# Cross attention in a six-layer kernel: V mixed for twelve chunks at a time, K stacked in pieces of 512 keys

## The reference

```python
Q = _proj(layernorm(x), Wq, bq)          # 256 x 16 x 32
K = _proj(ctx, Wk, bk); V = _proj(ctx, Wv, bv)   # 25088 x 16 x 32
scores = jnp.einsum('bihd,bjhd->bijh', Q, K) * SCALE
attn = jax.nn.softmax(scores, axis=1)    # over the 256 queries, for each key and head
x = jnp.einsum('bijh,bjhd->bihd', attn, V).reshape(B, S, D_MODEL)
return x @ Wo + bo
```

## Time and profile before

| | |
|---|---|
| median of 3 runs | 2509.08 us (2507.33 to 2509.38) |
| profiled execution | 2507.43 us |
| its span | 2505.7 us |
| granted TensorE clock, mean | 0.999 |
| PE busy | 2474.8 us, 99% |
| DVE, ACT, POOL busy | 77%, 73%, 48% |
| 16 DMA engines, SP's queue | 65.0% |

### The profile page before, as it was taken

How to read it: one execution, slowest core, us unless ns; L and a number is a source line. 1 busy time by engine, 2 the same in 40 slices (tenths; PEclk the granted TensorE clock), 3 DMA queues, 4 the chain that set the end, 5 groups by cost and what they waited for, 6 DMA issues and landing times.

```text
span 2505.7 us, 53166 instructions
## 1 busy us (share of the span) xinstructions
PE 2474.8 (99%) x18114; PEld 1993.9 (80%) x18114; DVE 1940.5 (77%) x3672; ACT 1827.4 (73%) x6877; POOL 1204.4 (48%) x1973
## 2 busy tenths in 40 slices
PE   8999999999999999999999999999999999999998
PEld 6876999877777777777777777777777777588897
DVE  8886866587778788877878777778788887669855
ACT  2214444288888888888888888888888888649743
POOL 5533111265555656555555565565556554430022
PEclk9999999999999999999999999999999999999999
DMA  9995545567676666766766776676676666348751
GB/s 391 386 373 212 196 185 190 130 175 171 167 171 165 165 164 163 176 162 164 174 161 166 170 169 167 163 169 166 163 178 163 163 156 136 152 162 333 289 200 44
DMA packets 138033, 472.98 MB, mean 189 GB/s; under 512 B 32664, under 2 KB 32792, under 8 KB 126368
## 3 DMA queue, kind: packets, MB, share of 16 engines
q1 hardware_dynamic: 130512, 456.20, 65.0%
q10 hardware_dynamic: 7248, 13.37, 1.4%
HBM read 244.53 MB, written 17.30 MB: 104 GB/s over the span
## 4 chain that ended last, share of the span: by engine, by line
PE 95%; DVE 2%; ACT 1%; DMA 1%; issue 0%; POOL 0%; SPq 0%; DVEq 0%
PE PB L816 21%; PE PB L846 15%; PE PB L834 14%; PE PB L857 14%; PE PB L776 6%; PE PB L622 6%; PE PB L956 4%; PE PB L971 3%; PE PB L789 3%; PE PB L1032 2%; PE PB L1058 2%; ACT EE L1264 1%; PE PB L665 1%; DMA AR<-in_ctx 1%; PE PB L722 1%; PE PB L672 1%
## 5 line engine op out<-in xcount | busy, mean ns | idle before, releaser
L1264 ACT ACTIVATE EE<-PB,small 128x256 f32<-128x256 f32 x3136 | 1435.8, 498 | 205.0 <-DVE small L1711 196.9
L1711 DVE TENSOR_REDUCE small<-PB 128x2 f32<-128x512 f32 x1568 | 1028.4, 683 | 314.5 <-PE PB L846 310.8
L1264 ACT ACTIVATION_READ_ACCUMULATOR EE<-PB,small 128x1 f32 x3136 | 721.3, 230 | 0.0
L846 PEld LDWEIGHTS PB<-QS,STK 128*128 128x128 f32 x3136 | 557.7, 188 | 175.0 <-issue 44.4
L816 PE MATMUL PB<-CTX,WKV 128*128 128x512 f32 x2352 | 680.8, 394 | 0.0
L2116 POOL TENSOR_TENSOR VS<-V,small 128x128 f32<-128x128 f32 x784 | 331.3, 423 | 676.1 <-DVE small L1717 676.1
L846 PE MATMUL PB<-QS,STK 128*128 128x256 f32 x3136 | 617.1, 285 | 3.2 <-ACT EE L1264 3.0
L834 PE MATMUL PB<-WKV,CTX 128*128 128x512 f32 x1584 | 469.2, 393 | 0.0
L816 PEld LDWEIGHTS PB<-CTX,WKV 128*128 128x128 f32 x2352 | 385.0, 189 | 29.7
L857 PE MATMUL PB<-EE,VS 128*32 128x256 f32 x6272 | 367.4, 381 | 1.0 <-POOL VS L2116 1.0
L857 PEld LDWEIGHTS PB<-EE,VS 128*32 128x32 f32 x6272 | 189.5, 110 | 131.3 <-POOL VS L2116 2.8
(11 more groups left out here) (287 smaller groups left out, 2385.3 us busy)
## 6 DMA issues: line engine op xcount, KB each, us to landing
STK<-KHL SPq DMA_DIRECT2D x1568, 128.0 KB, 2.4
RW<-in_l1f SPq DMA_DIRECT2D x64, 1024.0 KB, 5.7
AR<-in_ctx SPq DMA_DIRECT2D x49, 1024.0 KB, 8.2
RAW<-in_ctx SPq DMA_DIRECT2D x98, 512.0 KB, 3.8
WF<-in_l0f SPq DMA_DIRECT2D x17, 2304.0 KB, 9.0
V<-v_scr SPq DMA_DIRECT2D x64, 256.0 KB, 3.0
v_scr<-RAW ACTq DMA_DIRECT2D x49, 256.0 KB, 7.4
RW<-in_l1a SPq DMA_DIRECT2D x1, 4096.0 KB, 13.5
```

The lines of the kernel that those rows point to most:

```text
L846: m = e.matmul(bank(2 * (k % 2) + half, 256 * (s % 2), 256), STK[:, g % 2, s, c % 2, j:j + 128], QS[:, s, c, :], start=True, stop=True)
L1264: m = e.activation(EE[:, b, s, :], bank(2 * (k % 2) + half, 256 * (s % 2), 256), ACT.Exp, bias=nm[:, b, s:s + 1], accum_out=su[:, b, s:s + 1])
L1711: e.tensor_reduce(nm[:, k % RING, 2 * half:2 * half + 2], bank(2 * (k % 2) + half).rearrange("p (s i) -> p s i", s=2), axis=AX.X, op=ALU.m ...
```

## The change

Three things are changed together.

1. MIX goes from 6 to 12 and RING from 8 to 14. There is a batch of mixes after every twelfth chunk, and one more, of what is left, at the last chunk before TAIL.
2. K is no longer stacked in pairs: KHL, STK and KR hold one unit where they held two (KHL and STK still two in turn, KR one). `stack_k` runs for each unit, at k % 4 == 3, with 16 DMAs of half the size. Units are projected two ahead instead of four, and the context is loaded and split one group of 256 keys later. `k_raw` waits for the low part of the unit just before it.
3. OT and WO have no place of their own any more: OT lies in a slot of EE, WO in four slots of V, and W_o's load waits for V's last reader there. The last 16 chunks run in the plain order (`LAST_ORDER` goes), and the late V projections in `LATE_V` are moved some chunks forward.

```diff
-MIX = 6
-RING = 8
+MIX = 12
+RING = 14
...
-HEADS_DONE = [LAST + LAST_ORDER.index((3, c1 - 1)) + 1 for c0, c1 in HEADS_OUT]
+HEADS_DONE = [LAST + 4 * c1 for c0, c1 in HEADS_OUT]
+BATCH_ENDS = [k for k in range(TAIL) if k % MIX == MIX - 1 or k == TAIL - 1]
...
-    if k < LAST:
-        return 4 * (k // 16) + k % 4, k % 16 // 4
-    j, c = LAST_ORDER[k - LAST]
-    return NT - 4 + j, c
+    return 4 * (k // 16) + k % 4, k % 16 // 4
...
-    u = (k + AHEAD) // 4 + 4
+    u = (k + AHEAD) // 4 + 2
...
-        KHL = sb("KHL", [P, 2, 2, 2, CW], F32R, life)
-        STK = sb("STK", [P, 2, 4, 2, CW], F32R, life)
+        KHL = sb("KHL", [P, 2, 2, CW], F32R, life)
+        STK = sb("STK", [P, 2, 4, CW], F32R, life)
...
-        KR = sb("KR", [P, 2, CW], over=life)
+        KR = sb("KR", [P, CW], over=life)
...
+        OT, WO = EE[:, (NCH - 14) % RING], V[:, 4:8, :]
...
-            def stack_k(g):
-                if g >= 2:
-                    w.wait_ge("s_mm", 16 * (g - 2) + 16)
+            def stack_k(u):
+                if u >= 2:
+                    w.wait_ge("s_mm", 8 * (u - 2) + 8)
                 for part in range(2):
-                    w.wait_ge(*k_done(g, part))
+                    w.wait_ge(*k_done(u, part))
                     for s in range(4):
                         for q in (part, part + 2):
                             e.dma_start(
-                                STK[32 * q:32 * q + 32, g % 2, s, :, :].bitcast(F32),
-                                KHL[32 * s:32 * s + 32, g % 2, part, :, :].bitcast(F32)).then_inc(S[f"d_s{g % 2}"], 16)
+                                STK[32 * q:32 * q + 32, u % 2, s, :].bitcast(F32),
+                                KHL[32 * s:32 * s + 32, u % 2, part, :].bitcast(F32)).then_inc(S[f"d_s{u % 2}"], 16)
...
-                if k % 8 == 7 and g + 2 < NG:
-                    stack_k(g + 2)
-                if k % 8 == 5 and g + 7 < NG:
-                    load_ctx(g + 7)
+                if k % 4 == 3 and k // 4 + 2 < 2 * NG:
+                    stack_k(k // 4 + 2)
+                if k % 8 == 5 and g + 6 < NG:
+                    load_ctx(g + 6)
...
-            w.wait_ge("d_s1", 256 * NPAIR)
+            w.wait_ge("vs", NCH - 16)
...
-                first, last = k % MIX == 0, k % MIX == MIX - 1
+                first, last = k == 0 or k - 1 in BATCH_ENDS, k in BATCH_ENDS
...
-                if k % MIX == MIX - 1:
-                    for n in range(max(k - MIX - 1, 0), k - 1):
+                if last:
+                    for n in range(mixed, k - 1):
                         mix(n)
+                    mixed = k - 1
...
-                if (k + AHEAD) % 8 in (2, 3, 4, 5) and (k + AHEAD) // 8 + 4 < NG:
-                    split_lo((k + AHEAD) // 8 + 4, ((2, 3, 4, 5).index((k + AHEAD) % 8),))
+                if (k + AHEAD) % 8 in (2, 3, 4, 5) and (k + AHEAD) // 8 + 3 < NG:
+                    split_lo((k + AHEAD) // 8 + 3, ((2, 3, 4, 5).index((k + AHEAD) % 8),))
```

More of the change, by code:

```diff
@@ L388, in build, with k_done @@
         qf = EE[:, 3].rearrange("p c i -> p (c i)")
-        nm, su, rc = (small[:, o:o + 4 * RING].rearrange("p (b s) -> p b s", b=RING) for o in (0, 32, 64))
-        KBANK = (6, 7, 6, 3)
+        nm, su, rc = (small[:, o:o + 4 * RING].rearrange("p (b s) -> p b s", b=RING) for o in (0, 64, 128))
+        KBANK = (6, 7)
         VBANK = {1: 7, 2: 6}
-        def k_done(g, part):
-            return (("k_hi", "k_lo")[part], 2 * g + 2) if g < 2 else (("kr_hi", "kr_lo")[part], (1, 2)[part] * (2 * (g - 2) + 2))
+        def k_done(u, part):
+            return (("k_hi", "k_lo")[part], u + 1) if u < 2 else (("kr_hi", "kr_lo")[part], (1, 2)[part] * (u - 1))
         WS1 = (WSA, WSB)
@@ L840, in scores @@
                 t, c = chunk(k)
-                g, j = 2 * (t // 4) + c // 2, 128 * (t % 4)
-                w.wait_ge(f"d_s{g % 2}", 256 * (g // 2 + 1))
+                u, j = 4 * (t // 4) + c, 128 * (t % 4)
+                w.wait_ge(f"d_s{u % 2}", 256 * (u // 2 + 1))
                 if k >= 2:
@@ L845, in scores @@
                 for s in (2 * half, 2 * half + 1):
-                    m = e.matmul(bank(2 * (k % 2) + half, 256 * (s % 2), 256), STK[:, g % 2, s, c % 2, j:j + 128],
+                    m = e.matmul(bank(2 * (k % 2) + half, 256 * (s % 2), 256), STK[:, u % 2, s, j:j + 128],
                                  QS[:, s, c, :], start=True, stop=True)
@@ L884, in project @@
                 if u and steps:
-                    if steps[0] == 0 and u > 4:
-                        w.wait_ge("kr_out", u - 4)
+                    if steps[0] == 0 and u > 2:
+                        w.wait_ge("kr_out", u - 2)
                     project_k(u, steps=steps)
@@ L1254, in k_hi @@
                 w.wait_ge("kp_mm", u + 1)
-                e.activation(KHL[:, u // 2, 0, u % 2, :], bank(KBANK[u]), ACT.Identity,
+                e.activation(KHL[:, u, 0, :], bank(KBANK[u]), ACT.Identity,
                              bias=BC[:, C_L1XK + u:C_L1XK + u + 1]).then_inc(S["k_hi"], 1)
@@ L1270, in scalar_program @@
             move_xt(3)
-            for u in range(2, 4):
-                k_hi(u)
-                w.wait_ge("q_split", 1)
-                stack_q(e, 3, ((0, 1), (2, 3))[u - 2])
+            w.wait_ge("q_split", 1)
+            stack_q(e, 3, range(4))
             for k in range(NCH):
@@ L1690, in k_lo @@
                 e.scalar_tensor_tensor(
-                    out=KHL[:, u // 2, 1, u % 2, :], in0=bank(KBANK[u]), scalar=BC[:, C_L1XK + u:C_L1XK + u + 1],
-                    in1=KHL[:, u // 2, 0, u % 2, :].bitcast(F32), op0=ALU.add, op1=ALU.subtract).then_inc(S["k_lo"], 1)
+                    out=KHL[:, u, 1, :], in0=bank(KBANK[u]), scalar=BC[:, C_L1XK + u:C_L1XK + u + 1],
+                    in1=KHL[:, u, 0, :].bitcast(F32), op0=ALU.add, op1=ALU.subtract).then_inc(S["k_lo"], 1)
             def k_raw(u):
-                n, ch = u - 4, u % 4
+                n, ch = u - 2, u % 4
                 w.wait_ge("kp_mm", u + 1)
-                if n >= 2:
-                    w.wait_ge("kr_lo", 2 * (n - 1))
-                e.tensor_scalar(KR[:, n % 2, :], bank(4), BC[:, C_L1XK + ch:C_L1XK + ch + 1], None,
+                if n >= 1:
+                    w.wait_ge("kr_lo", 2 * n)
+                e.tensor_scalar(KR[:, :], bank(4), BC[:, C_L1XK + ch:C_L1XK + ch + 1], None,
                                 ALU.add).then_inc(S["kr_out"], 1)
@@ L1746, in vector_program @@
             e.tensor_tensor(hl[1], qf, hl[0].bitcast(F32), ALU.subtract).then_inc(S["q_split"], 1)
-            for u in range(2, 4):
-                k_lo(u)
-            split_hi(3)
             for n in range(3):
                 v_out(n)
-            split_hi(4, (0,))
+            split_hi(3, (0,))
             for k in range(NCH):
@@ L1766, in vector_program @@
                     e.tensor_tensor(X[:, k - 8, :], X[:, k - 8, :], BI[:, BSLOT[R_XO], :], ALU.add).then_inc(S["x_xbias"], 1)
-                if (k + AHEAD) % 8 in (0, 4) and (k + AHEAD) // 8 + 4 < NG:
-                    split_hi((k + AHEAD) // 8 + 4, ((0, 4).index((k + AHEAD) % 8),))
+                if (k + AHEAD) % 8 in (0, 4) and (k + AHEAD) // 8 + 3 < NG:
+                    split_hi((k + AHEAD) // 8 + 3, ((0, 4).index((k + AHEAD) % 8),))
             reciprocals(NCH - 1)
```

32 lines of the change are left out of this document (10 added, 22 removed).

## The result

The changed kernel takes 3033.84 us (median of 4 runs, 3028.98 to 3036.14) against 2508.35 us for the kernel before beside it: 1.209 times as long, 95% interval 1.207 to 1.211. It is 21% slower. The forecast was 3060 us in a range of 2540 to 3235. The profiled execution has a span of 3031.6 us.

A forecast was written before the change was run, and what follows sets the result against it. SP's queue of DMA issues was taken to bound: from 471.6 its 2219 us of work end near 2691; landing and the last four chunks give hand-over at 2708; adding 350.5 and 1.7 gives 3060 us, range 2540 to 3235.

The forecast's parts named there:

- rival B: On SP's queue an issue's cost follows its bytes, leaving ACT's lag of 45 us: 2552 us (2540 to 2580), chance 0.13.
- SP's queue becomes the bound: In the steady stage SP's issues take 11.3 us a unit against TensorE's 8.46; main case, 3060 us, chance 0.70.
- An issue costs 0.68 us whatever it moves: Each of 16 K issues a unit costs 0.68 us despite halved bytes; 196 stacks on SP take 2132 us.
- the 93 loads of context: Context loads on SP's queue in the loop, at 0.46 us each: 43 us of SP's 2219.
- the 32 pairs of V: Pairs of V issues on SP's queue, at 1.12 us each: 36 us of SP's 2219.
- the way from its last issue to the hand-over: After SP's last issue: landing, then the last four chunks (14.9 us) and about 1 us from a cold start; hand-over 2708.
- SP never waits (20.0 us against 22.7): Scores that free a stack slot end 20.0 us after that stack began, before two stacks' 22.7, so SP's queue never runs dry.
- The rarer switch, 20 us: TensorE switches into and out of mixes half as often: 64 x 0.31 = 20 us gained if nothing else is late.
- ACT's lag, 45 us net: Across a twelve-chunk mix ACT's exps fall behind TensorE's scores: 0.7 us a batch, 45 us slower with the switch's gain inside.
- The context and V splits later, "priced at nothing": VectorE's and GpSimd's splits move closer to use, at least 2 chunks (4.2 us) before the first V projection: no cost.
- C's 2487: TensorE stays the bound, with cheap issues and ACT keeping up: 2507.4 - 20 = 2487 us, chance 0.08.
- rival D: TensorE's idling on SP lowers its granted clock; 4166 us if low throughout, time above 3235 us, chance 0.07.

The follow-up runs named there:

- the run with all issues: The changed kernel with all its 16 issues a unit, only the context split two chunks sooner: 3025.80 us, ratio 1.207.

## Why the prediction was right

The range of 2540 to 3235 held rival B as well, so that the time fell into it says little. What was tested is the 3060 and the queue behind it.

**SP's queue becomes the bound: right.** It carries 56% of the chain, TensorE waits at the first scores of a unit 2.9 us each for the DMA where it waits (about 3 were named, for every unit; over all units it is 2.2), and ACT's share fell to 0.68 (about 0.65 was named). Quartering the issues takes 455 us away, quartering the bytes 13.

**An issue costs 0.68 us whatever it moves: right, a little high.** Between SP's first issue at 469.45 and its last end at 2663.04 lie 2193.6 us, where the prediction had 2219. Counted from the start of one issue to the start of the next, Q's 12 issues and the pause before them take 10.8, the 93 loads of context 62 and the 32 pairs of V 42. That leaves 2079 us for 196 stacks, 10.61 each, 0.663 an issue. The prediction had 10.88 for a stack: the term is 53 us smaller. The loads are 19 us dearer and V's pairs 6, because the prediction priced them as in the kernel before, where SP's queue has pauses (a load at 0.46 us); in a full queue a load takes 0.66 us to the next issue, as a piece of K does. These differences, with the pause of 2.8 us, are 25 of the 26 us between 3060 and 3034; SP's start, 2 us sooner, and the way from its last issue to the hand-over, 18.0 us and not 17, leave the last one. That errors of 53 and 28 us partly cancel is luck. The Trainium skill, "DMA: Bandwidth & Descriptors", section "Anatomy of one DMA", has about 50 ns for the sequencer's dispatch. That section describes the path of DMAs that GpSimd issues, and dispatch is one of several parts there, so the prediction's 0.8 us for 16 issues on SP does not follow from it. The runs have 591 to 599 ns an issue on SP's queue in four sizes, and 496 on GpSimd's.

One argument for this price did not hold, though its conclusion did. The prediction read V's 514 ns and the loads' 339 in the kernel before as a sign that bytes do not count. But V's issues follow directly behind a stack there, and more than half of the loads come after a pause. SP's queue in the kernel before, from the two V's of the earlier trace rows at 1214.10 on:

```profile
1216.01 0.33 SPq L484 DMA_DIRECT2D RAW<-in_ctx  x1
1221.94 11.40 SPq L504 DMA_DIRECT2D STK<-KHL  x16
1233.39 0.58 SPq L484 DMA_DIRECT2D RAW<-in_ctx  x1
```

The load after 0.84 us of pause takes 0.33 us, the one right behind a stack 0.58. Of the loads in its steady stage, the 25 that follow another issue directly have 580 ns in the median and the 34 after a pause about 335. The medians of the earlier trace rows differ by place. That bytes do not count was shown by the run with a quarter of them.

**SP never waits (20.0 us against 22.7): right in the changed kernel, with no room.** It waits 3.5 us of 1000 with the mix of twelve, and 31.5 with the mix of six. The margin of 2.7 us was worked out for TensorE at full clock, and the granted clock was 0.92; 5 waits for a unit's scores, 1.7 us of the 3.5, are this margin used up.

**The rarer switch, 20 us, and ACT's lag, 45 us net: invisible here, and mis-sized as a constant.** Behind the queue the mix of twelve is worth 42 us in favour. With issues out of the way it costs 18 us beside a late context split and 60 beside an early one. The mechanism (the scores at the end of a batch wait for the exps) was the one forecast, but its size changed with the place of the context split, which the prediction did not have. The switch itself, 0.31 us, was confirmed from the other side by the mix of five: 7.6 us for 26 more.

**The context and V splits later, "priced at nothing": wrong, and hidden.** The plan's margin of two chunks (4.2 us) before the V projection is not enough once in 24 chunks: 19 waits of up to 1.4 us in 1000 us. Taking them away gave 29 us with the mix of six, and the rest of the change beside issues and mix costs 53 in all. That did not touch the result, since TensorE waits for SP's queue far longer than this; for the split the run with all issues shows it, for the other 24 us it is argued. With a quarter of the issues and the mix of twelve the time is 2579, 27 us above rival B's 2552, and C's 2487 is out too: the change is then still slower than before.

**The clock (rival D): fell, and decided nothing.** The granted clock is 0.92 in the steady stage. With 8 or 4 issues a unit it was 1.00. After the wait of 5 us the scores and projections take up to twice as long for some 4.5 us, and TensorE then has that much less to wait for the next stack. SP's queue waits 1.7 us of 1000 for TensorE's scores, so little of this can have reached the time.

## What to carry to other kernels

Count the DMA issues of a queue, not only bytes and busy shares: issues per period times the start-to-start time in the trace, against the period of the engine that bounds. Halving a block that must be copied in a fixed number of pieces doubles that count, and past the edge they set the time (448 us between 8 and 16 a unit, 7 between 4 and 8). A price set at nothing because something larger covers it should be kept as a number, since it comes back when the cover is lifted; and a queue that has been relieved until it just fits will show the next late producer at once.

## What the runs showed of the hardware

An issue of a copy from SBUF to SBUF took 591 to 599 ns in the median on SP's queue with 16, 64, 128 or 256 KB and with 32, 64 or 128 partitions. Much depended on whether SP's queue had been idle. In the steady stages, after a pause of more than 1 us, a copy's issue took 507 ns in the median with 32 partitions (the kernel before), 462 with 64 (half of the issues) and 465 with 128 (a quarter), and a load of 128 partitions from DRAM 338 (the kernel before). Directly behind another issue the copies took 591 to 602 in these runs and the changed kernel, and the loads 580 to 590. In the full queue of the changed kernel, with the DMA engines half busy, pieces of K, loads and V's tiles all took 0.65 to 0.66 us from one start to the next, the long ones included. So an issue for a queue that will be full is to be priced by issues that stand directly behind others. GpSimd's queue took 496 ns for the same copy. What the queue does in this time was not tried.

At the same traffic (159 and 160 GB/s) copies of 64 partitions kept the DMA engines busy 0.66 of the time and copies of 128 partitions 0.45.
